# Letting GpSimd's gathers run without waiting for VectorE in the radial stage of a four-layer graph network

## The reference, cut to what matters

```python
x = _layernorm(x + _L0_gnn_ref(x, edge_weight, edge_attr_3, edge_index, w1, b1, w2, b2))
x = _layernorm(x + _L1_gnn_ref(x, edge_index))
x = _layernorm(x + _L2_gnn_ref(x, edge_index, edge_attr_32, ...))
x = _layernorm(x + _L3_gnn_ref(x, edge_attr3_2x32, src, dst, ...))
```

```python
src, dst = (edge_index[0], edge_index[1])
R = jax.nn.relu(abs_distances[:, None] @ w1 + b1) @ w2 + b2
Y = spherical_harmonics(rel_vec)
Fj = features[src]
...
acc = acc + _NORM[i] * jnp.einsum('euv,ef,evi,ofi->euo', Rb[..., k], Yf, Fb, C)
...
out = out.at[dst].add(msg)
```

## Time and profile before

| | us |
|---|---|
| median of 3 runs | 2275.79 (2261.41 to 2276.19) |
| the profiled execution, device time | 2269.11 |
| its span, first to last instruction | 2266.9 |
| outside the span (2269.11 - 2266.9) | 2.2 |
| radial stage, first feature product to last message write | 199.29 to 690.0 |
| GpSimd's gathers of this stage (line 672) | 135.12 to 736.6 |
| next layer's first gather (line 758) | 780.69 |

### The profile page before, as it was taken

The page is one execution under the profiler, slowest core; times in us unless marked ns, Lnnn a source line. Parts: engine busy times, 40 slices in busy tenths (PEclk is TensorE's granted clock), DMA queues, the critical chain, the costliest instruction groups (busy, mean ns, idle before and its releaser), DMA issues.

```text
span 2266.9 us, 14390 instructions
## 1 busy us (share of the span) xinstructions
PE 1028.1 (45%) x3772; PEld 691.5 (31%) x3772; DVE 1271.8 (56%) x2708; ACT 487.2 (21%) x951; POOL 1316.4 (58%) x1251
## 2 busy tenths in 40 slices
PE   7704835653630127142151067867446667601222
PEld 3202312321210127132141034434236667501121
DVE  9835947889836727850437923534744676703610
ACT  7522201110100215130122112222112223301100
POOL 8874566671777154277230266766166667773775
PEclk9955555555555658666565555555555555555555
DMA  7164311110101213130122300000000000100000
GB/s 289 31 220 142 110 18 27 27 26 11 28 13 46 79 26 124 56 102 25 53 96 94 114 3 3 19 11 12 25 17 21 22 24 22 28 12 7 9 12 8
DMA packets 69465, 114.07 MB, mean 50 GB/s; under 512 B 34205, under 2 KB 54026, under 8 KB 68602
## 3 DMA queue, kind: packets, MB, share of 16 engines
q1 hardware_dynamic: 24306, 80.74, 10.2%
q0 software_dynamic: 39104, 12.88, 4.4%
q10 hardware_dynamic: 5960, 19.43, 2.3%
HBM read 64.18 MB, written 55.21 MB: 53 GB/s over the span
## 4 chain that ended last, share of the span: by engine, by line
DVE 16%; PE 13%; another core or an unknown queue 13%; issue 11%; POOL 2%; ACT 2%; DMA 1%; DVEq 0%; ACTq 0%; POOLq 0%; SPq 0%
PE bank L1145 3%; DVE work L1381 3%; PE bank L1293 3%; PE bank L1286 3%; PE bank L1318 1%; DVE stat L1392 1%; DVE A_dst L1381 1%; DVE A_sum L1480 1%; POOL A_msg L758 1%; PE bank L1341 1%; POOL A_src L672 1%; DVE A_msg L1381 1%; DVE r L1392 1%; DVE A_sum L1389 1%
## 5 line engine op out<-in xcount | busy, mean ns | idle before, releaser
L672 POOL DMA_INDIRECT A_src<-table,pos_i x392 | 429.6, 1096 | 356.3 <-DMA table<-A_dst 164.4
L1220 PE MATMUL bank<-w2fold,work 65*128 65x384 f32 x392 | 270.4, 866 | 188.9 <-DVE work L1381 124.5
L1392 DVE TENSOR_REDUCE work<-work 128x80 f32<-128x1280 f32 (+3 forms) x147 | 204.8, 1424 | 125.9 <-issue 96.0
L672 POOL DMA_INDIRECT A_dst<-in_x,dst_i x196 | 203.9, 1040 | 107.6 <-issue 65.5
L811 POOL DMA_INDIRECT out<-A_dst,out_i x196 | 197.7, 1009 | 98.7 <-issue 62.1
L1220 PEld LDWEIGHTS bank<-w2fold,work 65*128 65x128 f32 x392 | 121.9, 329 | 335.6 <-issue 335.5
L1257 PE MATMUL bank<-nodes_w,small 128*128 128x128 f32 (+1 forms) x784 | 135.8, 341 | 184.7 <-ACT small L931 111.9
L1381 DVE TENSOR_TENSOR work<-bank,work 128x384 f32<-128x384 f32 (+1 forms) x294 | 155.0, 594 | 111.9 <-remote 77.0
L672 POOL DMA_INDIRECT A_src<-x_pos,A_tmp x140 | 144.5, 1032 | 89.8 <-issue 47.8
L1257 PEld LDWEIGHTS bank<-nodes_w,small 128*128 128x128 f32 (+1 forms) x784 | 125.2, 249 | 194.9 <-ACT small L931 119.7
L907 ACT ACTIVATE work<-A_tmp,b1col,w1col 65x256 f32<-65x256 f32 x98 | 58.7, 600 | 430.1 <-PE bank L1220 195.6
(11 more groups left out here) (354 smaller groups left out, 2216.0 us busy)
## 6 DMA issues: line engine op xcount, KB each, us to landing
work<-in_x SPq DMA_DIRECT2D x26, 960.0 KB
x_pos<-A_sum SPq DMA_DIRECT2D x13, 990.0 KB
out<-work ACTq DMA_DIRECT2D x13, 960.0 KB
A_tmp<-ew_turned_rows ACTq DMA_DIRECT2D x49, 130.0 KB
table<-A_dst SPq DMA_DIRECT2D x2, 3136.0 KB
edge_sums<-A_dst SPq DMA_DIRECT2D x2, 3136.0 KB
table<-A_dst SPq DMA_DIRECT2D x14, 448.0 KB
A_src<-table,pos_i POOLq DMA_INDIRECT x392
```

The source lines that it names most:

```text
L672: pool.indirect_dma_start(out=column(t), out_offset=None, in_=of, in_offset=bass.IndirectOffsetOnAxis(ap=idx[:, t:t + 1], axis=0), bounds_ ...
L1220: last = nc.tensor.matmul(banks[2 + 2 * slot + j][:, 0:PATHS], hidT[:, slot, j * P:(j + 1) * P], w2fold[:], start=True, stop=True)
L1392: return v.tensor_reduce(out=o, in_=a, axis=AX, op=op)
```

## The change

`keep_to_radial` and its constants go; the position, source and destination gathers that used it are issued without a wait for VectorE. `keep_to_histogram`, the waits for stored tables (`pos_stored`, `x_stored`, `zeros_stored`), the order of the gathers and all the other engines' programs stay.

```diff
@@ -76,7 +76,6 @@
-SLACK_PAIRS, PAIRS_CAP = 14, 84
@@ -676,7 +675,7 @@
-            issued = {"hist": 0, "radial": 0}
+            issued = {"hist": 0}
@@ -685,14 +684,7 @@
-            def keep_to_radial():
-                issued["radial"] += 1
-                k = issued["radial"]
-                need = min(int(0.37 * k) - SLACK_PAIRS, PAIRS_CAP)
-                if k % 4 == 0 and need > 0:
-                    pool.wait_ge(prod_used, need + SLOTS)
-
-            def gather_dst(columns, keep):
+            def gather_dst(columns, keep=None):
@@ -704,14 +696,13 @@
             pool.wait_ge(pos_stored, 32)
-            gather(lambda t: pos_x[:, t:t + 1], pos_table, src_i, node_limit, lambda t: pos_rows, range(plain),
-                   keep=keep_to_radial)
+            gather(lambda t: pos_x[:, t:t + 1], pos_table, src_i, node_limit, lambda t: pos_rows, range(plain))
...
             gather(lambda t: src_wide[:, t, :], x_pos, src_i, node_limit, lambda t: src_rows[t // GATHER_CHUNK],
-                   range(plain, T), keep=keep_to_radial)
-            gather_dst(range(DST_FIRST * GATHER_CHUNK, T), keep_to_radial)
+                   range(plain, T))
+            gather_dst(range(DST_FIRST * GATHER_CHUNK, T))
```

## The result

The changed kernel takes 2373.57 us (median of 4 runs, 2371.26 to 2397.66). The kernel before, in runs beside it, takes 2268.60 (2254.68 to 2276.19). The ratio is 1.049 with a 95% interval of 1.045 to 1.053, or 105 us: slower, as forecast, inside the range, and 40 us less than the 2414 predicted. The profiled execution took 2371.46 us against 2269.11. Its mean granted clock is 0.557 against 0.563, and in the radial stage it is 0.50 (1.2 GHz) in both.

A forecast was written before the change was run, and what follows sets the result against it. GpSimd's unbroken gathers were taken to starve the other engines in the radial stage. The stage's +160 us and -15 behind it made +145, so 2269.1 + 145 = 2414 us, range 2345 to 2465.

The forecast's parts named there:

- The mechanism: Radial stage: after about 36 us of unbroken GpSimd gathers, other engines get about one instruction per 1.4 us until a pause.
- TensorE's stalls are its own: Rival, radial stage: GpSimd's pauses are result, not cure; only the 15 us behind the stage return, 2254 us; chance 0.06.
- Half as slow: Rival, radial stage: slow pairs take 7 us instead of 11.2, giving 2354 us; chance 0.12.
- The idle window gets used: Rival: 32 gathers move into GpSimd's 42.17 us idle around make_short, giving 2235 us, faster by 1.5%; chance 0.06.
- Start, +9: Ahead of the radial stage: chunk 0 begins at about 208 instead of 199.3, 9 us later, bounds 0 and +15.
- Gathers, 411.6 us: Radial stage: 140 + 168 gathers run unbroken from 254.3 for 411.6 us, to 666.
- Pairs beside them, 57: Radial stage: 24 pairs done before the slow phase at 290.3, 33.5 more at 11.2 us, 57 when gathers end.
- The rest, 4 + 143 + 37 = 184: Radial stage after the gathers: 4 us recovery, 41 pairs at 3.49 for 143, make_short 37; stage ends at 850.
- +160: The radial stage ends at 850 instead of 690, 160 us later, with the later start of 9 included.
- Behind the stage, -15: Stretch from 690.02 to 777.94: with GpSimd silent, 15 of 20 us idle come back, bounds 0 and 20.
- 145: Whole kernel: +160 in the stage and -15 behind it, 145 us slower on the profiled execution, 2414 us.
- The queue: TensorE's 64-instruction queue, 8 per 2.9 us out, 1 per 1.4 in, drains in about 31 us; not in the sum.

The follow-up runs named there:

- GpSimd's own pauses: Changed kernel, GpSimd waiting for its own last gather to land before every seventh row gather: 2255.79 us, ratio 0.987 to the kernel before (chip A).
- the second profile: The changed kernel, unedited, run again on chip B: 2398.30 us, ratio 1.051 to the kernel before.
- positions free: Pacing removed for the 56 position gathers alone, the 308 row gathers still paced: 2318 us beside 2301 for the kernel before (chip A).
- the longer period: Changed kernel with one GpSimd memset ahead of each row gather: 2242.72 us, ratio 0.983 to the kernel before (chip A).
- half the matmuls: Changed kernel with one matmul per bank pair left out: 2330.54 us, ratio 1.018 on chip B; 1893.12 us, ratio 1.000 on chip C.
- The same kernel with ten pauses: Changed kernel, GpSimd waiting for its own last gather before every 28th row gather: 1907.95 us, ratio 1.004 on chip C; 2365.90, 1.035 on chip B.
- after 14: Changed kernel, GpSimd pausing before every 14th gather from chunk 0's destination gathers on, 28 destination gathers moved earlier: 2179.04 us, ratio 0.949 (chip B).

## Why the prediction was right, and where its terms were off

*The mechanism.* Unbroken row gathers starve the other engines at one instruction per 1.40 us: right, on the chips that have it. What supplies the instructions stays open. Seen: no gap of GpSimd's between 231 and 638, products 11.20 apart with waits on "remote" and "issue", an unchanged clock, make_short only behind the gathers and 37.17 us long, chunk 6 in 48.56, and the slow phase 37 us behind the resumption, where I had put 36. One reading beside it was wrong: I set TensorE's matmuls of 662.97 against VectorE's products of 672.42, but by the program's order they belong to those of 683.61. The spacing of 11.2, which the sum used, is not touched by it. The rival that TensorE's stalls are its own falls with GpSimd's own pauses. "Half as slow" falls with the two chunks at 156.80. "The idle window gets used" needed pairs under 6 us and had 11.2.

*Start, +9.* This is the step that failed. Chunk 0 began at 151.59, 48 us earlier than before's 199.29 and not 9 later. VectorE's small instructions ahead of it ran clean, and the slow phase came inside chunk 0 instead, which took 82.24 us. Of the 48 us 14 were left when x_pos was stored: GpSimd went on at 231.40, against 245.34 before and 254.3 predicted. The cause stays open. The instructions issued until then are the same in both kernels, as the waits removed come later. Chance from one execution to the next is unlikely but not excluded: the second profile, on chip B, has chunk 0 at 151.62 and the resumption at 232.78. And it is not the removed position waits alone. Four other kernels without them, three on chip A and one on B, did what I had worked out, chunk 0 near 208 and the resumption near 254.3: positions free 206.99 and 258.91, own pauses before every seventh 206.97 and 259.05, the longer period 207.83 and 259.04, half the matmuls 205.47 and 255.14. When a slow phase sets in thus shifts by tens of microseconds between kernels that are alike in that stretch.

*Gathers, 411.6 us.* They took 407.0, and with the earlier resumption ended at 638.35 instead of 666: 27.7 less.

*Pairs beside them, 57.* 56 were done at 620.21, and 18.1 / 11.2 = 1.6 more by 638.35. The count came out right although two of its parts did not, since the slow chunk 0 took back what the early start gave.

*The rest, 4 + 143 + 37 = 184.* It took 190.5 (638.35 to 828.86). The recovery is mis-sized, as it is not over after 4 us: products at 647.40, 657.20 and 663.53, some 25 us until full speed. The one row that I took the 4 from the earlier trace rows was of ScalarE behind a shorter run.

The stage so ended 138.8 us later than before, where +160 was predicted: -27.7 and +6.5.

*Behind the stage, -15.* From the stage's end to the next layer's first gather before took 90.7 us and after 73.4: -17.3. The difference at that gather is +121.6, and it shrinks from there without a cause that I can show: +116.7 at the first gather of the attention stage (1401.23 against 1284.57), +110.2 at the next (1743.25 against 1633.08), +102.4 at the end. Nothing there was changed; I had said that nothing later changes but its start, and those 19 us (121.6 to 102.4) are the rest of the 43 by which 145 was too much on the profiled execution; the first 23 are the stage's and those behind it.

*The queue.* I had noted that the Trainium skill's queue of 64 instructions ("TensorE: Matmul & The Clock Gate", Architectural detail) would drain in about 31 us. That estimate took TensorE at its pace inside a pair, 8 instructions per 2.90 us; over whole pairs it takes 8 per 3.49, and the same estimate from the page's 64 becomes 41 us, and about 150 with half the matmuls. The onset was 37 us and, with half the matmuls, 65: later, as something that TensorE's own pace helps to drain would have it, but not by this depth. Nor do the other runs fit one depth: on chip C nothing drained in 440 us of the same gathers beside half the matmuls, and with a period of 1.38 us the onset was some 200 us away. No run shows the queue itself.

## What to carry to other kernels

When an engine's idle time is ended by "remote" or "issue" and its instructions stand a constant time apart, divide a stretch by each engine's instruction count: two stretches with different counts and one quotient (here 1.40 and 1.38 us) show that instructions, not operations, are what is short. A pacing wait can be worth its place for the pause alone; ask whether the engine could pause for itself, often and briefly, instead of rarely and at length. Measure such a change on more than one chip, since here the same kernel was 3.5% slower than before on one and level on another.

## What was not expected of the hardware

- Between chips: before took 1897 us on one chip and 2269 to 2301 on the others. The same kernel with ten pauses had chunks of 48.5 us on the first and of up to 156.1 on another, with GpSimd's gathers at 1.30 us and the granted clock at 0.50 in both. What differs in the chips is not in any record here.
- In the slow phase beside gathers every 1.30 us each engine gets one recorded instruction per 1.40 us: TensorE's 112 a chunk made 156.80 us, VectorE's 68 made 93.79 (1.38 each), and 27 small ones of VectorE without any of TensorE's made 35.68 (1.32 each). Beside gathers every 1.38 us, in make_short, it was 0.66 us on average.
- A pause refills only a share: 1.7 us after 7 gathers kept the supply up for the whole stage, after 14 nearly (chunks of 48.5 to 53.1), after 28 it did not, and the loss grew from 6 to 107 us a chunk.
- A memset between gathers, which lengthened their period from 1.30 to 1.38 us, kept three chunks clean and a fourth within 3 us.
